# A decoder layer on one core: gates in two groups, and attention's last batches moved between the first units of the mLSTM

## The reference, cut to what matters

```python
x = x + attention(layernorm(x))              # 16 heads of 16, causal softmax, output projection
x = x + mlstm(layernorm(x), ctx, ctx)        # 8 heads of 32
x = x + moe(layernorm(x))                    # 8 experts, top 2, exact gelu

# inside mlstm, for q = layernorm(x), k = v = ctx
pre = 15 * tanh((concat(q, k, v) @ ifgate_w.T + ifgate_b) / 15)
i_pre, f_pre = pre[..., :8], pre[..., 8:]
lf = cumsum(log_sigmoid(f_pre))                       # along the 256 tokens
log_d = lf[t] - lf[s] + i_pre[s]   for s <= t         # else -inf
m = max over s of log_d;  d = exp(log_d - m)
s_mat = (q k^T / sqrt(32)) * d
h = (s_mat @ v) / (max(|sum s_mat|, exp(-m)) + 5e-5)
h = h * rsqrt(mean(h*h) + 1e-6) * (1 + outnorm_w)
```

## Time and profile before

| what | value |
|---|---|
| median of three runs | 1018.48 us |
| the profiled execution | 1012.4 us |
| its span, first to last instruction | 1010.6 us |
| PE, DVE, ACT, POOL busy in the span | 878.4, 610.7, 478.8, 529.1 us |
| mean granted TensorE clock | 0.948 of full |

### The profile page before, as it was taken

How to read it: one execution, slowest core, us unless ns; L and a number is a source line. 1 busy time by engine, 2 the same in 40 slices (tenths; PEclk the granted TensorE clock), 3 DMA queues, 4 the chain that set the end, 5 groups by cost and what they waited for, 6 DMA issues and landing times.

```text
span 1010.6 us, 31607 instructions
## 1 busy us (share of the span) xinstructions
PE 878.4 (87%) x11871; PEld 657.3 (65%) x11960; DVE 610.7 (60%) x1326; ACT 478.8 (47%) x798; POOL 529.1 (52%) x664
## 2 busy tenths in 40 slices
PE   4898898989897427999899889899999999999995
PEld 3566666766665314666666577687777878787783
DVE  3776677777665333677777766655555555555553
ACT  3556666766666324656555444233333333333331
POOL 2545655654656324458788776743435343444342
PEclk8999999999999658989989899999999999999998
DMA  9112343234234543436546323343323333333322
GB/s 282 46 32 66 82 104 111 75 86 135 76 85 116 136 134 108 146 113 187 161 151 182 121 84 84 80 93 48 51 47 52 48 50 49 50 52 49 50 28 28
DMA packets 132718, 92.97 MB, mean 92 GB/s; under 512 B 74848, under 2 KB 113632, under 8 KB 132448
## 3 DMA queue, kind: packets, MB, share of 16 engines
q1 hardware_dynamic: 119280, 73.10, 26.4%
q0 software_dynamic: 13296, 17.83, 10.7%
HBM read 54.65 MB, written 37.32 MB: 91 GB/s over the span
## 4 chain that ended last, share of the span: by engine, by line
PE 59%; DVE 12%; ACT 8%; POOL 6%; DMA 6%; issue 4%; SPq 1%; POOLq 0%; DVEq 0%; ACTq 0%
PE pair L876 18%; PE pair L890 10%; PE pair L892 7%; PE pair L609 4%; PE pair L623 3%; POOL sm L1439 3%; PE pair L587 3%; DMA o_scr<-On 2%; PE pair L636 2%; DMA STG<-wup_in 2%; PE pair L842 1%; PE pair L767 1%; DVE SD L1061 1%; PE pair L793 1%; ACT PT L1237 1%
## 5 line engine op out<-in xcount | busy, mean ns | idle before, releaser
L876 PE MATMUL pair<-XTs,WU 128*128 128x128 bf16 x3408 | 285.6, 221 | 11.1 <-DVE XTs L1184 4.8
L876 PEld LDWEIGHTS pair<-XTs,WU 128*128 x3408 | 239.0, 98 | 79.0 <-issue 16.2
L1474 POOL DMA_INDIRECT out_d<-XB x71 | 115.3, 1624 | 207.9 <-DVE XB L1206 178.3
L1351 ACT ACTIVATE Hf<-pair 128x512 f32<-128x512 f32 x142 | 84.8, 597 | 223.2 <-PE pair L876 223.1
L890 PE MATMUL pair<-WD,Hh 128*128 x479 | 182.1, 381 | 0.1
L1197 DVE CAST Hh<-Hf 128x512 bf16<-128x512 f32 x142 | 63.4, 446 | 170.7 <-ACT Hf L1351 170.6
L892 PE MATMUL pair<-WD,Hl 128*128 x568 | 155.3, 274 | 4.7
L1396 POOL TENSOR_SCALAR_AFFINE_SELECT PT<-PT 128x512 f32<-128x512 f32 (+1 forms) x96 | 74.4, 789 | 61.2 <-ACT PT L1237 55.7
L1199 DVE TENSOR_TENSOR Hl<-Hf,Hh 128x512 bf16<-128x512 f32 x142 | 99.7, 702 | 4.9
L962 DVE TENSOR_REDUCE mxn<-pair 128x4 f32<-128x1024 f32 x64 | 75.3, 1218 | 25.9 <-PE pair L568 25.9
L1061 DVE TENSOR_TENSOR SD<-pair,SD 128x1024 f32<-128x1024 f32 x48 | 58.6, 1221 | 40.7 <-ACT SD L1306 22.6
(11 more groups left out here) (234 smaller groups left out, 1785.7 us busy)
## 6 DMA issues: line engine op xcount, KB each, us to landing
XB<-xs_scr SPq DMA_DIRECT2D x71, 130.0 KB, 2.1
STG<-wup_in SPq DMA_DIRECT2D x32, 256.0 KB, 4.8
q_scr<-SPL SPq DMA_DIRECT2D x16, 512.0 KB, 4.0
STG<-wdn_in SPq DMA_DIRECT2D x32, 256.0 KB, 3.6
o_scr<-On SPq DMA_DIRECT2D x32, 128.0 KB, 4.1
Mm<-o_scr SPq DMA_DIRECT2D x16, 256.0 KB, 2.9
CnT<-ctxt_in SPq DMA_DIRECT2D x16, 256.0 KB, 4.4
CX<-ctx_in SPq DMA_DIRECT2D x16, 256.0 KB, 3.1
```

Source lines behind the costliest of these rows:

```text
L876: t = e.matmul(upb(j, k)[:, 128 * (fm % 4):128 * (fm % 4) + 128], WU[:, bass.ds(reg[j] * 4096 + off, 128)], XTs[:, r, hx, dk, :], start=n ...
L1351: e.activation(Hf[:, r, hs], upb(j, k), ACT.Gelu).then_inc(gel.sem, 1)
L1474: e.indirect_dma_start(out=out, out_offset=bass.IndirectOffsetOnAxis(ap=XS[:, i % NX, 256:257].bitcast(I32), axis=0), in_=Yf[:, i % NY, :] ...
```

## The change

The gates are made in two groups of eight batches, on 64 partitions each. Group 0 (steps Gt, GT, Gs, GE, Gp, Go) runs within attention's rounds 13 to 16. Attention's rounds end at 16; then SP fetches the mLSTM's first inputs ("in" for batches 0 and 1), PE does PV and A4 of batch 15 between the two, and the mLSTM begins. What attention's rounds 17 to 21 did (gate sums of batches 12 to 15, layer norm, transposes and splits of 13 to 15, the addition of 14 and 15) stands in the dictionary `rest` between the units of rounds 0 to 2, and group 1's gates between those of rounds 2 and 3. All PE steps of `rest` use the one bank `tb`, in turn with B4 and B5 (`tb_free`). Both meetings of the engines are gone. Chunks 32 to 35 of the expert weights are no longer split between the stages but in the mLSTM's rounds, two in nearly every round. Buffers in SBUF are laid out anew so that the mLSTM's buffers lie on those that attention has done with; the memsets of `LR`, `WD` and `Q1` follow the last T2. The part of `g_scr` that holds ones is written once at the start by three more DMAs.

```diff
-    for i in range(-2, B + 6):
+    for i in range(-2, B + 1):
...
+        if i == 14:
+            yield "GT", 0, 0
+        if i == 15:
+            yield "Gp", 0, 0
+            yield "Go", 0, 0
...
         if ok(i - 1):
             yield "T0", i - 1, 1
+        if i == 14:
+            yield "Gs", 0, 0
...
-        if i > B and ok(i - 2):
-            yield "A4", i - 2, 0
...
+        if i == 13:
+            yield "Gt", 0, 0
+        if i == 14:
+            yield "GE", 0, 0
...
+    yield "in", 0, 0
+    yield "PV", B - 1, 0
+    yield "A4", B - 1, 0
+    yield "in", 1, 0
...
-    pend, ready, chunk, sent, part = [], 0, 36, 0, 0
+
+    pend, ready, chunk, sent, part = [], 0, 32, 0, 0
+    z = B - 1
+    rest = {(0, 0): (("GA", z - 3), ("A6s", z - 2), ("Mm", z), ("X1", z - 1), ("A6n", z - 2), ("A6c", z - 2)),
+            (0, 1): (("A6s", z - 1), ("XQ", z - 2), ("A6n", z - 1)),
+            (0, 2): (("A6c", z - 1), ("X1", z), ("A6s", z), ("GA", z - 2)),
+            (1, 0): (("XQ", z - 1), ("A6n", z)), (1, 1): (("A6c", z), ("GA", z - 1)), (1, 2): (("XQ", z),),
+            (2, 0): (("GA", z), ("Gt", 1)), (2, 1): (("GT", 1),), (2, 2): (("Gs", 1),),
+            (3, 0): (("GE", 1),), (3, 1): (("Gp", 1),), (3, 2): (("Go", 1),)}
     for i in range(B):
-        for _ in range(3 if i == B - 1 else 1 + (i % 3 != 0)):
+        for _ in range(3 if i == B - 1 else 1 if i == 2 else 2):
...
+            for kind, b in rest.get((i, u), ()):
+                yield kind, b, 0
...
+        tb_users = [s[:2] for s in bsteps if s[0] in ("X1", "XQ", "GA", "GT", "GE", "B4", "B5")]
+
+        def tb_free(w, kind, b):
+            i = tb_users.index((kind, b))
+            if i == 0:
+                pair_left(w, 3)
+                return
+            kind, b = tb_users[i - 1]
+            if kind == "X1":
+                w.wait_ge(x1_.sem, x1_.at(b))
+            elif kind == "XQ":
+                w.wait_ge(qnl.sem, qnl.at(b))
+            elif kind == "GA":
+                w.wait_ge(ga_.sem, ga_.at(b))
+            elif kind == "GT":
+                w.wait_ge(g_dve.sem, g_dve.at("gg", b))
+            elif kind == "GE":
+                w.wait_ge(g_dve.sem, g_dve.at("em", b))
+            elif kind == "B4":
+                w.wait_ge(hh_.sem, hh_.at(b))
+            elif kind == "B5":
+                w.wait_ge(x3h.sem, x3h.at(b))
...
+        def vector_gate_scans(e, w, q, ps):
+            w.wait_ge(g_act.sem, g_act.at("ln", q))
+            w.wait_ge(g_pe.sem, g_pe.at("emT", q - 1))
+            w.wait_ge(p_init.sem, p_init.at("z"))
+            e.tensor_tensor_scan(cs_, gf, zfill[0:64, 0:256], 0.0, ALU.add, ALU.add).then_inc(g_dve.sem, 1)
+            w.wait_ge(g_dve.sem, g_dve.at("cs", q))
+            e.scalar_tensor_tensor(gg_[:, :], ps[0:64, 0:256], 15.0, cs_, ALU.mult, ALU.add).then_inc(g_dve.sem, 1)
+            w.wait_ge(g_dve.sem, g_dve.at("gg", q))
             e.tensor_tensor_scan(MM[:, :], gg_[:, :], gg_[:, :], NEG, ALU.max, ALU.max).then_inc(g_dve.sem, 1)
-            w.wait_ge(g_dve.sem, g_dve.at("MM"))
-            e.tensor_tensor(cs_[:, :], cs_[:, :], MM[:, :], ALU.subtract).then_inc(g_dve.sem, 1)
-            w.wait_ge(g_dve.sem, g_dve.at("run"))
+            w.wait_ge(g_dve.sem, g_dve.at("MM", q))
+            e.tensor_tensor(cs_, cs_, MM[:, :], ALU.subtract).then_inc(g_dve.sem, 1)
+            w.wait_ge(g_dve.sem, g_dve.at("run", q))
             e.tensor_scalar(MM[:, :], MM[:, :], -1.0, None, ALU.mult).then_inc(g_dve.sem, 1)
-            w.wait_ge(g_dve.sem, g_dve.at("neg"))
-            for q in range(3):
+
+        def vector_gate_ends(e, w, q, ps):
+            w.wait_ge(g_pe.sem, g_pe.at("emT", q))
+            e.tensor_scalar(EM[:, :, gate_rows(q)], ps[:, 0:128].rearrange("p (t c) -> p t c", t=2), 5e-5, None, ALU.add).then_inc(g_dve.sem, 1)
...
+        def vector_gate_parts(e, w, q):
+            w.wait_ge(l_g, 32 * q)
+            w.wait_ge(g_dve.sem, g_dve.at("neg", q))
+            w.wait_ge(g_pe.sem, g_pe.at("emT", q))
+            for n in range(3):
...
+        def scalar_gates(e, w, kind, q, ps):
+            if kind == "Gt":
+                w.wait_ge(ga_.sem, ga_.at(8 * q + 7))
+                e.activation(G[:, :, :, gate_rows(q)], G[:, :, :, gate_rows(q)], ACT.Tanh, scale=1.0 / 15.0).then_inc(g_act.sem, 1)
+            elif kind == "GT":
+                w.wait_ge(g_pe.sem, g_pe.at("T", q))
+                w.wait_ge(g_dve.sem, g_dve.at("pp", q - 1))
+                e.activation(gf, ps[0:64, 256:512], ACT.Exp, scale=-15.0).then_inc(g_act.sem, 1)
+                w.wait_ge(g_act.sem, g_act.at("exp", q))
+                e.activation(gf, gf, ACT.Ln, bias=1.0).then_inc(g_act.sem, 1)
+            else:
+                w.wait_ge(g_dve.sem, g_dve.at("run", q))
+                e.activation(cs_, cs_, ACT.Exp).then_inc(g_act.sem, 1)
...
+                    if b >= 43:
+                        for k in range(2):
+                            w.wait_ge(l_sp[k], 16 * B // 2)
+                        w.wait_ge(l_g, 64)
+                        w.wait_ge(l_z, 32)
...
+            w.wait_ge(t2m.sem, t2m.at(B - 1, 1))
+            e.memset(LR[:, :, :, :, :].rearrange("p r x k c -> p (r x k c)").bitcast(F32), 0.0).then_inc(lr_z, 1)
             for q in QS:
                 e.memset(q[:, 0:2048].bitcast(F32), 0.0).then_inc(qb_z, 1)
...
+                elif kind == "Go":
+                    gates_out(e, w, b)
+                elif kind == "in":
+                    decays(e, w, b)
+                    queries(e, w, b)
+                    contexts(e, w, b)
...
+        def gates_out(e, w, q):
+            w.wait_ge(g_dve.sem, g_dve.at("pp", q))
+            for k in range(2):
+                e.dma_start(gsc[6 * k:6 * k + 3, gate_rows(q), :].rearrange("k p c -> p k c"), pp[:, 3 * k:3 * k + 3, :]).then_inc(l_g, 16)
...
-        def sync_gates(e, w):
-            load_chunk(e, w, 32)
-            load_chunk(e, w, 33)
-            for b in range(2):
-                queries(e, w, b)
-                contexts(e, w, b)
-            w.wait_ge(g_dve.sem, g_dve.at("pp"))
-            e.dma_start(gsc.rearrange("k p c -> p k c"), pp[:, :, :]).then_inc(l_g, 16)
-
         def sync_mlstm(e, w):
-            for b in range(2):
-                decays(e, w, b)
-            load_chunk(e, w, 34)
-            load_chunk(e, w, 35)
...
+                elif kind == "Mm":
+                    merged(e, w, b)
+                elif kind == "XQ":
+                    queries_out(e, w, b)
+                elif kind == "A6c":
+                    if b + 1 < B:
+                        contexts_t(e, w, b + 1)
+                elif kind == "Go":
+                    gates_out(e, w, b)
```

398 lines of the change are left out of this document (218 added, 180 removed).

## The result

The changed kernel is slower. Over 20 runs each it took 1023.83 us (median; 1016.24 to 1030.08) against 1017.40 (1012.14 to 1021.21) for the kernel before: a ratio of 1.0060, 95% interval 1.0042 to 1.0078. A later series (6 runs against 17) gave 1.0087 (1.0052 to 1.0122). The forecast was 1016, 2.6 us faster; 1023.8 lies in the range and on the other side of zero: the change costs 6.4 us where a gain of 2.6 was forecast. The profiled execution took 1020.87 us with a span of 1019.1, against 1012.4 and 1010.6.

What follows compares the result with a forecast made beforehand. PE stands idle 44.9 us between attention and the mLSTM; the start keeps 31.7 after attention's 7.0, and 31.7 - 16.6 - 12.5 = 2.6 gained. 1018.5 - 2.6 = 1015.9, say 1016 us; range 1001 to 1028.

Steps and rivals of the forecast that it cites:

- Group 0 within attention: 7 us lost: Attention's rounds 14 and 15: group 0's gate steps delay reduces and exponentials by 7.0 us, bounds 3 and 12.4.
- The remark that half the partitions are no cheaper: DVE's five small gate instructions work on 256 columns whatever the partitions, so they still take 4.4 us.
- The start, (0,0) at 345.5: Start of the mLSTM: ACT's exponential of batch 0, unit 0 comes at 345.5 instead of 377.22, a lead of 31.7 us.
- Rounds 0 and 1: 16.6 lost: mLSTM rounds 0 and 1: waits for chunks, contexts and norms take 16.6 us of the lead, bounds 13 and 20.
- Rounds 2 and 3: 12.5 lost: mLSTM rounds 2 and 3: group 1's gates and waits for shared bank `tb` take 12.5 us, bounds 7 and 18.
- Chunks in rounds 6, 9 and 12: at nothing: mLSTM rounds 6, 9 and 12: one more chunk to split each costs nothing, or 3.6 us if POOL has no room.
- Rival 1: Waits overlap more: attention grows by 3, rounds 0 and 1 lose 14, rounds 2 and 3 lose 7; 1004 us, chance 0.27.
- Rival 2: Units (0,1) to (1,1): ACT waits for late chunks and contexts, PE idles at a lower clock; slower, 1025 us, chance 0.22.
- its mark of 359.6: In the mLSTM's start: chunk 32 landing after 359.6, with nothing made up, loses 2.6 us more and decides for slower.
- Rival 3: ACT's four table switches cost a drain of 1.38 us each as well, 5.5 in all: 1021.4 us, chance 0.06.
- Rival 4: Across all engines' lists: a hidden meeting of the engines is left; the prediction saw nothing for it and gave no chance.
- What the profile would show: Signs: batch 15's PV ends near 338, first `LR` matmul near 345, waits for `STG`, `hh` and Gs, (4,0) near 420.

Runs made afterwards that it cites:

- Run 9: Changed kernel with the transposes of batch 13's merged heads moved behind the last scores of batch 15 in attention's last round: 1.0031 of the kernel before.
- run 2: Changed kernel with group 0's steps at other places of attention's rounds 14 to 16: 0.9966 of the kernel before.
- Run 1: Changed kernel with SP issuing the loads of chunks 32 and 33 ahead of batch 0's mLSTM inputs: 0.9986 of the kernel before.
- run 3: Changed kernel with group 1's chain a round later and the shared bank freed before the scans: 1.0062 of the kernel before.
- run 8: Changed kernel without group 1's gates, batches 8 to 15 using those of batches 0 to 7: 0.9977 of the kernel before.
- run 14: Against a version with steps spread and loads reordered (0.9801): one chunk instead of two in rounds 6 and 9, three in 13 and 14; 0.9824 of the kernel before.

## Why the prediction was wrong, point by point

**Group 0 within attention: 7 us lost. This is the step that failed.** It measured 12.5 and 11.8, at the upper end (12.4) that the prediction had for "nothing is hidden". From one exponential to the next it went: T2(12) to T2(13) 4.8 us longer than before, to T2(14) 4.5 more, to T2(15) 3.2 more; the terms were 4.8, 2.2 and nothing. Round 14 was right in sum (`MT` 3.9 late), partly by luck: DVE's five instructions took 2.7 us and not 4.4, and the reduce came 2.7 late and not 5.5. The terms after it were not: `pp` (4.35 us on DVE, 313.25 to 317.60, where 3.1 was counted) was put at 0.7 on the path with the argument that ACT waits longer for a layer norm there, but that norm's statistics and the reduce stand behind `pp` on DVE, so its wait grew with it, and PE's wait for the reduce too; and the chain that leaves attention's engines, `On` to HBM and back to `Mm`, had no term at all. In the kernel before PE had not waited for it (`Mm` fetched at 318.19, transposed at 322.03); when round 15 came late, the round trip, which takes 333.84 - 325.04 = 8.8 us by this trace, came onto the path in front of the last scores. Run 9 prices that at 3 to 6, run 2 the places of all of group 0 at some 8. The remark that half the partitions are no cheaper was wrong for the scans: they took 0.73 and 0.68 us on 64 partitions against 1.48 and 1.69 on 128; the subtraction and the negation took 0.42 and 0.29 as before.

**The start, (0,0) at 345.5.** It came at 352.72. Attention's 5.5 explain most of it; the way from T2(15) to (0,0) shrank by 36.1 in place of 38.7. The 2.6 are four small terms: SP came to its eight `LR` issues 10.0 us behind T2(15) (346.53, behind batch 14's `Mm` at 345.08, `q_scr` and context) where the kernel before had 9.0; the issues took 3.3 in place of 2.7; D stood 1.7 behind their end and not 1.3; and the exponential 1.2 behind D. I had put 0.6 for that, though the rows of the kernel before had 377.22 - 375.97 = 1.25.

**Rounds 0 and 1: 16.6 lost.** Right: 16.0 and 15.8. ACT's wait for chunk 32 was 10.36 us, the first query norms waited for POOL, as written, and (0,1) stood 16.05 behind (0,0) where the chain had 16. Behind that two misses cancel by luck: (1,0) stood 4.7 behind (0,2) and not 2.9, (1,1) 5.5 behind (1,0) and not 7.5. Run 1 confirms the cause.

**Rounds 2 and 3: 12.5 lost.** Right in its mechanism, 10.5 and 11.0 in size; the 2 us less lie at (3,1), 5.0 behind (3,0) in place of 7.0. PE waits for `hh` in front of the last gate sums and again in front of GE, and for the second scan instruction's read of the shared bank. Runs 3 and 8 add that it is the chain's instructions that cost, not only the bank.

**Chunks in rounds 6, 9 and 12: at nothing.** Wrong; the bound of 3 x 1.2 = 3.6 was near the value: rounds 4 to 15 lost 3.0 and 5.3, the kernel before with these chunks 3.1, and run 14 finds 1.2 to 1.5 for each in its round. In the traces of the changed kernel, though, the time appears in rounds 7 and 12 (13.6 and 13.6, before 11.0 and 12.6) and not in 6 and 9, so the way by which a split costs is open. That PE is the busiest engine in a round doesn't cover work on ACT between two exponentials, since D of the next unit waits for each of them.

**Sum.** The forecast was -2.6. Attention gave 5.5 more, the way to (0,0) 2.6 more, rounds 0 to 3 2.6 less, rounds 4 to 15 3.0 more: +5.9; on the same chip +7.7. Two of these mis-sized terms had their value at a bound that the prediction itself wrote down: 12.4 for attention, of which it took 7.0 in the middle, and 3.6 for the chunks, of which it took nothing.

**The rivals.** Rival 1 (faster, 1004) is out: attention grew by 12 and not by 3, and the rounds lost 16.0 and 10.5 where it had 14 and 7. Rival 2 named the right sign and about the right time, 1025, but not the place, and that is luck: the start of the mLSTM lost what was forecast. Chunk 32 landed past its mark of 359.6, at 364.1, because (0,0) was 7.2 late itself, and the way from there was not longer. The lower clock that it names was there, 0.57 between 352 and 376 us, but rounds 0 and 1 lost no more than my chain without it. Rival 3, a drain with each table switch, is out: the Ln starts at 291.91, 0.01 us after a load of 1.28 that began at 290.62, and the exponential behind the load back 0.01 after it. The figure of the Trainium skill (ScalarE: Activation LUTs, What ACT_TABLE_LOAD costs), another 1.38 us to drain, doesn't show in any of the four switches. Rival 4 rightly had nothing.

**What the profile would show.** PV of batch 15 to end near 338: it ended at 342.7. `LR` near 345: 352. Waits for `STG`, `hh` and the scans: all seen. (4,0) near 420: 425.07. Of the prediction's signs one was met: D of (0,0) was late, 351.55, so the start was mis-sized, mostly by what attention gave it. Behind (4,0) the first pair of traces differs by 6.6 us and the second by -0.3; the 3.0 and 5.3 in rounds 4 to 15 are the part that repeats.

## What to carry to other kernels

Work put "within" a pipelined stage costs what stands behind it in its engine's list; here some 8 of 12 us were won back by the same steps at other places of the same three rounds, so place each step by the trace's gaps before judging the idea. When a stage is made later, look for the round trips through memory that were just hidden: they come onto the path without any instruction being added. Where a cost has two bounds and an instruction of it stands between two links of the chain that sets the end, start from the upper one; here it was the value in two such terms of four.

## What the runs showed of the hardware

- A scan over 256 columns took 0.73 and 0.68 us on 64 partitions, 1.48 and 1.69 on 128; but the same instruction on 64 took 1.13 in the trace of run 3, and a subtraction of 64x256 took 1.34 in two traces (314.17 in that of the changed kernel) and 0.42 in all others. What slowed them was not tried.
- The matmuls behind a wait can be slower. The same eight transposes of `OTs` took 1.97 us at 321.58, behind a wait of 3.9 of PE, and 1.06 at 343.95. The granted clock was 0.50 in the first stretch below and 1.00 in the second, the two levels of 1.2 and 2.4 GHz (kernel after, windows):

```profile
321.60:323.50 1.90, 1.90 (x13) 1.90 (x10) 1.65 (x3) 1.82 (x2) 1.81 (x3) 0.50 0.01 4
344.00:345.00 1.00, 1.00 (x8) 0.78 (x8) 0.00 (x0) 0.00 (x0) 0.01 (x1) 1.00 0.00 0
```

- The way of the heads through HBM, 5.7 us from the issue of the store (325.04) to that of the load (330.78) and 3.1 more until PE has them (333.84), is a link of 8.8 us in the kernel after. In the kernel before one such way took 8.0 (327.91, 332.57, 335.94).
- One kernel's stage of the experts, (15,2) to the end, took 441.2 and 448.3 us in two traces. A difference of 4 us between two single profiles says nothing there.
